# A twelve-layer decoder on one core: four groups of batches in turn instead of three, the SBUF for it taken from the value tile and the weight stream

## What is computed

```python
x = _layernorm(x + _L0_attn_ref(x, ...))              # "rec": a recurrence over the batch, solved ahead
x = _layernorm(x + _L0_xattn_ref(ctx_1024, x, ...))   # "x0": 16 heads of 8 channels
x = _layernorm(x + _L0_ffn_ref(x, gate_w, w1, w2))    # "f0": experts over chosen tokens
x = _layernorm(x + _L1_attn_ref(x, ...))              # "a1"
x = _layernorm(x + _L1_xattn_ref(x, ctx_1024, mask_BxS2_ik0, ...))   # "x1": with a key mask
x = _layernorm(x + _L1_ffn_ref(x, ...))               # "f1": rounded to FP4 levels
x = _layernorm(x + _L2_attn_ref(x, ...))              # "a2"
x = _layernorm(x + _L2_xattn_ref(x, ctx_1024, ...))   # "x2"
x = _layernorm(x + _L2_ffn_ref(x, ...))               # "f2"
x = _layernorm(x + _L3_attn_ref(x, ...))              # "a3"
x = _layernorm(x + _L3_xattn_ref(x, ...))             # "x3"
x = _layernorm(x + _L3_ffn_ref(x, ...))               # "f3": conv, attention, then 8 experts (128 -> 512 -> 128)
```

## Time and profile before

| what | value |
|---|---|
| median of 3 runs | 5131.43 us (5127.7 to 5132.52) |
| the profiled execution | 5134.53 us, span in the trace 5132.4 us |
| PE busy | 4564.4 us, 89% of the span |
| PEld busy | 3364.1 us, 66% |
| DVE busy | 3280.6 us, 64% |
| ACT busy | 2485.0 us, 48% |
| POOL busy | 780.2 us, 15% |
| mean granted clock of PE | 0.943 |

### The profile page before, as it was taken

The page is one execution under the profiler, slowest core; times in us unless marked ns, Lnnn a source line. Parts: engine busy times, 40 slices in busy tenths (PEclk is TensorE's granted clock), DMA queues, the critical chain, the costliest instruction groups (busy, mean ns, idle before and its releaser), DMA issues.

```text
span 5132.4 us, 128497 instructions
## 1 busy us (share of the span) xinstructions
PE 4564.4 (89%) x54601; PEld 3364.1 (66%) x54601; DVE 3280.6 (64%) x8433; ACT 2485.0 (48%) x5062; POOL 780.2 (15%) x841
## 2 busy tenths in 40 slices
PE   5668988999998989899898989899998989898877
PEld 4346756677676767677676767676676767676654
DVE  6655677656667575756667575757667585757552
ACT  3325645535545455555545454555545454554431
POOL 5551200101011110101111110101011111101000
PEclk7579989999999999999999999999999999999987
DMA  2122100012010101111010101011101101010000
GB/s 66 29 85 67 53 2 2 8 52 62 28 40 11 56 21 51 28 40 38 28 38 13 61 17 51 27 41 38 32 28 30 52 16 57 17 45 20 18 19 29
DMA packets 154183, 181.61 MB, mean 35 GB/s; under 512 B 62890, under 2 KB 82450, under 8 KB 152850
## 3 DMA queue, kind: packets, MB, share of 16 engines
q1 hardware_dynamic: 153618, 173.41, 11.4%
HBM read 162.50 MB, written 10.55 MB: 34 GB/s over the span
## 4 chain that ended last, share of the span: by engine, by line
PE 64%; DVE 15%; ACT 6%; issue 6%; POOL 2%; DMA 0%; SPq 0%; POOLq 0%; DVEq 0%; ACTq 0%
PE g_pair L2774 8%; PE g_pair L2759 8%; PE g_pair L1599 6%; DVE g_tops L1703 5%; PE g_pair L1649 5%; PE g_pair L1626 5%; ACT g_keys_exps L1679 4%; PE g_pair L1996 2%; PE g_pair L1986 2%; PE g_pair L1611 2%; PE g_pair L1433 1%; PE g_pair L1660 1%; PE g_pair L2060 1%; PE g_pair L2360 1%; PE g_pair L1569 1%
## 5 line engine op out<-in xcount | busy, mean ns | idle before, releaser
L1679 ACT ACTIVATE g_keys_exps<-g_pair 128x1024 f32<-128x1024 f32 (+1 forms) x768 | 747.8, 1018 | 587.2 <-PE g_pair L1626 585.9
L1703 DVE TENSOR_REDUCE g_tops<-g_pair 128x8 f32<-128x1024 f32 (+1 forms) x768 | 750.2, 1006 | 306.2 <-PE g_pair L1599 304.2
L1412 POOL TENSOR_TENSOR g_rstd<-g_rstd,minus_half 128x4 f32<-128x4 f32 x224 | 233.0, 1041 | 3305.4 <-DVE g_rstd L1394 3304.8
L2774 PEld LDWEIGHTS g_pair<-region,g_keys_exps 128*128 128x128 f32 x4096 | 511.3, 192 | 113.9 <-issue 104.3
L2774 PE MATMUL g_pair<-region,g_keys_exps 128*128 128x128 f32 x4096 | 548.6, 278 | 2.9 <-DVE g_base L2806 2.9
L2759 PE MATMUL g_pair<-g_xT,region 128*128 128x512 f32 x1024 | 545.6, 614 | 5.9 <-ACT g_keys_exps L2787 3.1
L1649 PE MATMUL g_pair<-g_keys_exps,g_v 77*32 77x128 f32 (+1 forms) x12288 | 437.8, 286 | 67.7 <-DVE g_tops L1703 58.6
L1626 PE MATMUL g_pair<-g_qa,g_keys_exps 32*77 32x128 f32 (+1 forms) x12288 | 448.6, 284 | 43.9 <-DVE g_o L1724 28.2
L1599 PE MATMUL g_pair<-g_keys_exps,g_qa 32*128 32x256 f32 (+1 forms) x6144 | 390.0, 368 | 99.9 <-ACT g_keys_exps L1679 80.2
L1626 PEld LDWEIGHTS g_pair<-g_qa,g_keys_exps 32*77 32x77 f32 (+1 forms) x12288 | 384.0, 170 | 143.9 <-DVE g_o L1724 62.1
L1649 PEld LDWEIGHTS g_pair<-g_keys_exps,g_v 77*32 77x32 f32 (+1 forms) x12288 | 328.0, 114 | 171.5 <-DVE g_tops L1703 117.6
(11 more groups left out here) (379 smaller groups left out, 8515.7 us busy)
## 6 DMA issues: line engine op xcount, KB each, us to landing
region<-L_w_in SPq DMA_DIRECT2D x512, 256.0 KB, 3.1
region<-xT_in SPq DMA_DIRECT2D x16, 256.0 KB, 2.8
z_scratch<-m_z SPq DMA_DIRECT2D x4, 1024.0 KB, 5.5
g_qa<-xT_in SPq DMA_DIRECT2D x16, 256.0 KB, 2.9
g_oT_sc<-z_scratch SPq DMA_DIRECT2D x64, 64.0 KB, 2.7
g_o<-x_in SPq DMA_DIRECT2D x16, 256.0 KB, 4.1
out<-g_x SPq DMA_DIRECT2D x16, 256.0 KB, 2.3
setup_weights<-prepared_in SPq DMA_DIRECT2D x1, 2589.5 KB, 11.0
```

The costliest lines, as they stand in the source:

```text
L1412: e.tensor_tensor(g.rstd[:, :], g.rstd[:, :], g.s["minus_half"], ALU.pow).then_inc(*b.gpsimd(st + " rstd"))
L1679: e.activation(g.p[0:nk, 2 * k:2 * k + 2, :, :].rearrange("p g u q -> p (g u q)"), b.pair[st][k][0:nk, :, :].rearrange("p r c -> p (r c)") ...
L1703: e.tensor_reduce(top_columns(g, k), src, AX, ALU.max).then_inc(*b.vector(f"{st} top {n} {k}"))
L2774: ins = e.matmul(bank[1][:, n * D:(n + 1) * D], g.gated_hid[:, x % 2, c, n * T:(n + 1) * T], weights.part(f"w2 {x}", c), start=c == n == 0 ...
```

## The change

Four groups instead of three: 16 batches are now four for each group. A fourth set of tiles needs SBUF, and the rest of the change makes room for it:

- `g.v` holds the heads h and h + 8 together in 48 columns (`VW = 48`): values of h at 0, a one at 8, values of h + 8 at 32, a one at 40. The matmul reads columns 0 to 31 for the one head and 16 to 47 for the other, so it is as wide as before.
- Streamed weights have three places a layer instead of four (`PLACES = 3`); the number of a piece now runs on over the batches.
- The key mask has no tile of its own any more. It is loaded into `g.o` when "f0 y" is done, not at the start of the batch, and POOL makes it ready between "f0 rstd" and the a1 stage.
- The scales of f1's rounding move into scratch; a mask used in the opening, and the last third of the opening's `W`, get other homes; `region` becomes smaller.
- The tiles' constant columns are set at the start of each group's POOL program instead of for all groups ahead of it.
- `ORDER` and `GIVEN` are written anew for four groups (the opening's `MEMORY_ORDER` is not changed). Each engine has the same instructions as before but for six more memsets on POOL, for the fourth group's constants; the 89 loads of an ACT table are as many too.

```diff
-VW = 32
+VW = 48
+PLACES = 3
-GROUPS = 3
+GROUPS = 4
...
 ORDER = {
     "tensor": (
-        "00010012021002020012201001000001010000202100101010112121211121221211121222101012012001200022000200100100"
+        "01010101010332230202110130101100010110100010111010001011010120120101212132302202022320032022200200202200"
...
-        self.key_mask_int, self.key_mask = sb("mask_int", 1, SEQS, S2, dt=I32), sb("mask", 1, SEQS, S2)
-        self.v = sb("v", P, SEQS, HEADS, VW)
+        self.v = sb("v", P, SEQS, HEADS // 2, VW)
+        self.key_mask = self.o[0:1, :, 0:S2]
+        self.key_mask_int = self.key_mask.bitcast(I32)
...
 def values_of(g, i):
 
-    return g.v[:, :, 8 * i:8 * i + 8, 16 * i:16 * i + HD]
+    return g.v[:, :, :, 32 * i:32 * i + HD]
...
-                ins = e.matmul(b.bank[st][0][32 * u:32 * u + 32, k * T:(k + 1) * T], g.v[0:nk, n, 8 * i + 4 * k + u, :],
+                ins = e.matmul(b.bank[st][0][32 * u:32 * u + 32, k * T:(k + 1) * T], g.v[0:nk, n, 4 * k + u, 16 * i:16 * i + 32],
...
-    held = [None] * 4
+    held = [None] * PLACES
     for b in batches:
-        for i, piece in enumerate(stream.pieces):
-            if held[i % 4]:
-                other, before = held[i % 4]
+        for piece in stream.pieces:
+            i = stream.number(b, piece) % PLACES
+            if held[i]:
+                other, before = held[i]
                 e.wait_ge(*other.tensor[read(before)])
...
+    e.wait_ge(*b.tensor["f0 y"])
+    e.dma_start(g.key_mask_int, dram["key_mask"][at].rearrange("b k -> (b k)").rearrange("(a b k) -> a b k", a=1, b=SEQS)
+                ).then_inc(g.arrived["mask"], 16)
+    yield
...
+def fixed_columns_gpsimd(e, g):
+
+    e.memset(g.tops[:, :], 0.0).then_inc(g.fixed, 1)
+    e.memset(g.xTp[:, :, 0:T + 2:T + 1], 0.0).then_inc(g.fixed, 1)
+    e.memset(g.small[:, :], 0.0).then_inc(g.fixed, 1)
+    e.memset(g.v[:, :, :, :], 0.0).then_inc(g.fixed, 1)
+    e.wait_ge(g.fixed, 4)
+    for i in range(2):
+        e.memset(g.v[:, :, :, 32 * i + HD:32 * i + HD + 1], 1.0).then_inc(g.fixed, 1)
+    yield
```

More of the change, by code:

```diff
@@ L270 @@
[L270 to L279, removed]
@@ L1995, in routed_tensor @@
             for c in range(HC):
-                ins = e.matmul(bank[half][:, i * P:(i + 1) * P], weights.part(f"w2 {x}", c), g.hid[:, x, c, :],
+                ins = e.matmul(bank[half][:, i * P:(i + 1) * P], weights.part(b, f"w2 {x}", c), g.hid[:, x, c, :],
                                start=c == 0, stop=c == HC - 1)
@@ L2758, in hidden @@
             e.wait_ge(*taken(k - 1))
-        e.matmul(bank[0][:, :], weights.part(f"w1 {x}", c), g.xT, start=True, stop=True).then_inc(*b.tensor(f"f3 hidden {k}"))
+        e.matmul(bank[0][:, :], weights.part(b, f"w1 {x}", c), g.xT, start=True, stop=True).then_inc(*b.tensor(f"f3 hidden {k}"))
         yield
@@ L2774, in gated_tensor @@
                 ins = e.matmul(bank[1][:, n * D:(n + 1) * D], g.gated_hid[:, x % 2, c, n * T:(n + 1) * T],
-                               weights.part(f"w2 {x}", c), start=c == n == 0, stop=c == HC - 1 and n == SEQS - 1)
+                               weights.part(b, f"w2 {x}", c), start=c == n == 0, stop=c == HC - 1 and n == SEQS - 1)
             if c < HC - 1:
@@ L2992, in loads_sync @@
     g, at = b.g, slice(first, first + SEQS)
-    if b.turn:
-        e.wait_ge(*b.gpsimd.before("key mask"))
-    e.dma_start(g.key_mask_int[:, :, :], dram["key_mask"][at].rearrange("b k -> (b k)").rearrange("(a b k) -> a b k", a=1, b=SEQS)
-                ).then_inc(g.arrived["mask"], 16)
-    yield
     e.dma_start(g.kq_dot[:, :], dram["s"][:, at]).then_inc(g.arrived["dots"], 16)
@@ L3053, in stream_sync @@
             at = int(x) * DFF
-            e.dma_start(stream.places[:, i % 4, :], dram[f"{stream.layer}_{w}"][:, at:at + DFF]
-                        ).then_inc(stream.arrived[i % 4], 16)
-            held[i % 4] = b, piece
+            e.dma_start(stream.places[:, i, :], dram[f"{stream.layer}_{w}"][:, at:at + DFF]
+                        ).then_inc(stream.arrived[i], 16)
+            held[i] = b, piece
             yield
@@ L3430, in _ @@
             def _(e):
-                for g in groups:
-                    e.memset(g.v[:, :, :, :], 0.0).then_inc(g.fixed, 1)
-                    e.memset(g.tops[:, :], 0.0).then_inc(g.fixed, 1)
-                    e.memset(g.xTp[:, :, 0:T + 2:T + 1], 0.0).then_inc(g.fixed, 1)
-                    e.memset(g.small[:, :], 0.0).then_inc(g.fixed, 1)
-                    e.wait_ge(g.fixed, 4)
-                    for i in range(2):
-                        e.memset(g.v[:, :, 8 * i:8 * i + 8, 16 * i + HD:16 * i + HD + 1], 1.0).then_inc(g.fixed, 1)
                 gpsimd_program(e, batches)
```

401 lines of the change are left out of this document (209 added, 192 removed), and 2 rows, old and new, of the table BATCH.

## The result

| kernel | median | runs |
|---|---|---|
| before | 5131.98 us (5127.7 to 5142.69) | 4 |
| changed | 5059.53 us (5053.15 to 5077.78) | 4 |

The ratio is 0.9856, 95% interval 0.9839 to 0.9873: the changed kernel is 1.4% or some 73 us faster. The profiled execution took 5053.15 us; its span is 5051.2 us, 81.2 us less than the 5132.4 of before. Lines of the changed kernel's profile stand 6 to 12 higher: scores L1605, turned tops L1617, shifted scores L1632, values L1655, exponentials L1685, tops L1709, the experts' matmuls L2770 and L2785, the loads L3066.

The account below looks back on a forecast made before the run. PE bounds the kernel, 92.8% busy in the middle, idle mostly in attention's waits and worse at the end. From the 5132.4 us span, -75 (end) -10 (start) +20 (places) -10 (middle) gave 5057, forecast as 5055; range 4950 to 5135.

Parts of the forecast that it names:

- The end: After the third last batch: lonely attention runs beside the second last batch's experts, 452 us become 179; gain 75 us.
- My second count: Gain at the end with moved work priced without experts, 183 us for 1315 instructions: 452 - 179 - 183 = 90 us.
- The start: First 728 us of the decoder phase: a fourth chain gives back 10 us, bounds 0 and 30.
- the middle: Full stretch of the decoder phase: cover inside attention nearly as before, a fourth group gains only 10 us.
- the fourth group fills the middle: Rival, 20%: stretches without experts come to 91% busy on PE, worth 130 us, time 4925.
- one turn of four groups: Sign in the middle: 4 x 282 to 285 us confirms its term; 275 or less, first rival; 290 or more, second.
- Three places: Streamed expert weights: w2 pieces land late, 21 x 1.3 = 27 us; taken as 20 us cost, bounds 0 and 146.
- Values, key mask, constants: Value matmuls and mask load cost 0, bounds 0 and 20; POOL's constants cost nothing, 2 us if their cover were gone.
- slower by the order's waves with the three places: Rival, 15%: the middle slows through DVE competition and late weight pieces, 5125 to 5192; decides from about 0.4 us a piece.
- Only the end, by the lower count: Rival, 15%: only the end moves, by 55 us, start and middle give nothing; some 5100 us.

Follow-up runs that it names:

- Half tops: DVE takes the largest scores of a2, a3 and f3 over half the keys: kernel before 5107.91 us (0.9936), changed kernel 5040.76 us (0.9807).
- added work: Every fourth hidden matmul of the last experts issued twice: kernel before 5240.79 us (ratio 1.0201), changed kernel 5172.06 us (1.0068).
- the pair of runs: Changed kernel with values packed in 34 columns a pair: three places 5064.83 us; four places, loads asked for one piece sooner, 5044.04 us.

## Why the prediction was right, point by point

The time was 5059.5 us for 5055 predicted. The sum was -75 - 10 + 20 - 10 = -75 against the span, which moved by -81.2. Its terms did less well than the sum: the end gave some 25 us more than I took and the start and the middle some 18 us less, and these two errors nearly cancel. That the total is within 5 us is luck in part.

**The end** was the largest term and had the right mechanism. Predicted: 452 us become 90 + 76.5 + 12.6 = 179; measured 84.9 + 73.0 + 12.6 = 170.5. Undoing the overlap of the last batch's chain alone cost 89 us and took all of the gain away. The price of the moved work was chosen as 198 us between 183 and 218. The trace gives 167.65 us of PE's busy time, 181.8 us at the share of the stretch it went to: the lower bound, as the argument about the right kind of work would have had it. So the term is 281.5 - 181.8 = 99.7 us for the 75 that I took, outside my bounds of 55 to 90. My second count, 90 us, had the right price; it is some 10 us below the 99.7, and 8.6 of them are the shorter new end: 84.9 for 90 and 73.0 for 76.5. The 73.0 are the last batch's experts, for which I took the time that they had at a granted clock of 0.89; at 1.00 PE is busy 62.37 us in them where it was 69.96.

The clock is also a larger part of the whole gain than the prediction says, though its sum held most of it: the old end went in at its measured 452 us, slow matmuls included, and the moved work at the middle's price. In the end of before PE was busy 355.3 us; now it is 84.56 + 62.37 = 146.9 us. Of the 208.3 us less only 167.65 came back before the end, and PE is busy 4516.5 us in all where it was 4564.4 (the 7.2 us that are left of that difference lie in the opening). In the old end the granted clock was 0.93, 0.63 and 0.89; in the new one it is 1.00 in both stretches. A lonely batch was slow twice, by its waits and by matmuls that took longer.

**The start** (-10) and **the middle** (-10) gave together about nothing: -81.2 + 99.7 - 20.8 (the places, below) leaves -2 us for both. In the first 728 us of the decoder phase PE is busy 647.81 us where it was 646.05. The decoder phase up to the third last batch was busy 92.2% and is 91.9%. That fits what the middle's small term rested on, that the cover inside attention is nearly the same with four groups. Half tops were worth about the same in both kernels (0.64% and 0.5%), and added work cost the same. The rival that the fourth group fills the middle (4925) is out: it asked for 91% in the stretches without experts, and they are at 88.8 and 86.7%. Why they are no fuller is not shown; that the four pairs of PSUM hold a fourth group back, as the prediction has it, was not tried.

The test that I had set, one turn of four groups at 4 x 282 to 285 us, can't be read from the times at which batches end, since they now end in waves (at 3521, 3823, 3948, 4053, 4536 and 4881 us). It can be read from PE's work. A batch is 788.85 / 3 = 262.95 us of it; from 1338 to 4880.7 us PE does 3278.13 / 262.95 = 12.5 batches' worth in 3542.7 us, 284 us for each, inside the 282 to 285. In the kernel before it was 283 (3357.51 in 3619).

The Trainium skill (Perfetto Trace Analysis, Identifying the Most-Contended Engine) says to judge the tensor engine's headroom by the share of its peak arithmetic that a kernel reaches and by the weight load's busy share. By the second, 69% in the middle, a third of PE's time would be free. The runs here bear the matmuls' share out instead: added hidden matmuls cost some three quarters or more of their own duration (103 of 138.7 us, 109 of 136.1).

**Three places** were sized at 20 us and cost 20.8 by the medians of the pair of runs (17 by their ratios), 18.5 by the sum of the windows. That the size came out so well is luck, for the place of the cost was wrong in part. I worked it out from 21 w2 pieces of the last experts at 1.3 us; the trace shows 5.8 us of waits there, six of some 1 us each, and 19.4 us on the first layer's lines, which I had given the rest of the 20 and no count. The mechanism can be seen in the last experts of the changed kernel, alone on PE:

```profile
4987.35 1.05 PE L2785 MATMUL g_pair<-region,g_keys_exps 128*128 128x128 f32 x8
...
4987.55 1.22 SPq L3066 DMA_DIRECT2D region<-L_w_in  x2
...
4990.61 1.13 PE L2785 MATMUL g_pair<-region,g_keys_exps 128*128 128x128 f32 x8 [1.06 <-DMA region<-L_w_in]
```

The request goes out when the hidden matmuls have read the expert's first piece, at 4987.55; the next matmul of the second weight starts 3.06 us later and had waited 1.06 us for the load. How the cost depends on the order is not settled: the kernel before pays 39 us for the same place, in an order of steps that was written for four places.

**Values, key mask, constants** at nothing: right for the layout (1.0001). The mask was not tried alone; no wait of POOL for its load stands in the trace, and the decomposition above leaves nothing for it.

The rival "slower by the order's waves with the three places" (it decides at 0.4 us a piece) was refuted by its own measure: 25.2 us of waits for loads over 224 pieces are 0.11 us a piece. "Only the end, by the lower count" (5100) was right about where the gain is and wrong about its size.

## What to carry to other kernels

When several chains take turns on a saturated engine, another chain was worth what the stretch with too few chains lost, and next to nothing where the engine was busy 92% already: compare the busy time of the end with the busy time that its work needs in the full stretch, the slower clock included, before you hope for the middle. A wait that repeats inside a chain moves to the next link when one link is shortened (88.6 to 33.3 us here, and 53.8 to 102.3 beside it), so cost the link behind it as well. A buffer taken away from a stream is paid in waits for its loads, and the same place can cost twice as much in another order of steps (21 and 39 us here): count them in every layer that uses the stream, not only where the cover looks thinnest (19.4 of 25.2 us were in the layer that I had not counted).

## What the runs showed of the hardware

The end's clock was a surprise. PE's granted clock in the lonely attention was 0.63, near the lower of its two levels (1.2 of 2.4 GHz is 0.5), and the last batch's experts began at it. The timeline of PE in the kernel before (start, duration, and x2 for the two records of one hidden matmul), with the same line 15 us later:

```profile
5046.26 2.04 PE L2759 MATMUL g_pair<-g_xT,region 128*128 128x512 f32 x2 [0.87 <-ACT g_keys_exps L2787]
...
5061.53 1.10 PE L2759 MATMUL g_pair<-g_xT,region 128*128 128x512 f32 x2
```

In the changed kernel the engine comes to the last batch's lonely experts out of 84.9 us in which it was busy for 84.56, and they start at full speed:

```profile
4967.58 1.10 PE L2770 MATMUL g_pair<-g_xT,region 128*128 128x512 f32 x2 [1.11 <-DVE g_keys_exps L2810]
```

The same waits of 0.9 to 1.1 us between these matmuls stand in both, so it is what came before that differs. Overlap in the end paid twice, and in the kernel whose end was undone the clock fell again, to 0.74 in the lonely stretch. The last batch's experts there (the same matmul, now L2942) begin slow and are at full speed 14 us later:

```profile
5064.22 2.04 PE L2942 MATMUL g_pair<-g_xT,region 128*128 128x512 f32 x2 [0.87 <-ACT g_keys_exps L2970]
...
5078.38 1.10 PE L2942 MATMUL g_pair<-g_xT,region 128*128 128x512 f32 x2
```
